# Macaron block (feed-forward, causal attention, feed-forward) on one core: evacuations moved from ScalarE to VectorE, and the last head's sums moved behind the next exponentials

## What is computed

```
x = x + 0.5 * ffn(layernorm(x))      # F1; weight rounded to -1, 0, 1 times its mean absolute value
x = x + attn(layernorm(x))           # softmax over the keys, causal
x = x + 0.5 * ffn(layernorm(x))      # F2
attn(x): kqv = x @ Wqkv + bqkv; scores = k q / sqrt(32), masked; softmax; @ v; @ Wo + bo
```

## Time and profile before

| | us |
|---|---|
| median of 3 runs | 1170.1 |
| lowest of them | 1168.0 |
| the profiled execution's own time | 1165.19 |
| its span, first to last instruction | 1163.4 |
| TensorE, ScalarE, VectorE, GpSimd busy | 1098.4, 930.6, 739.8, 344.1 |

### The profile page before, as it was taken

The page is one execution under the profiler, slowest core; times in us unless marked ns, Lnnn a source line. Parts: engine busy times, 40 slices in busy tenths (PEclk is TensorE's granted clock), DMA queues, the critical chain, the costliest instruction groups (busy, mean ns, idle before and its releaser), DMA issues.

```text
span 1163.4 us, 26100 instructions
## 1 busy us (share of the span) xinstructions
PE 1098.4 (94%) x9466; PEld 709.0 (61%) x9466; DVE 739.8 (64%) x2304; ACT 930.6 (80%) x2571; POOL 344.1 (30%) x471
## 2 busy tenths in 40 slices
PE   4688999999999999999999999999999999998896
PEld 3465655465666666675666666675666666664465
DVE  6766446479754666779754666779853666754344
ACT  1248889778998989878998989978998989989641
POOL 4731120135301232335301332335401332300253
PEclk9898989599999999999999999999999999999799
DMA  7432311111112121321112121321112111000021
GB/s 254 144 110 74 111 57 39 47 50 45 45 41 83 66 66 48 120 84 48 43 43 83 66 66 48 120 80 42 47 48 83 66 65 48 21 21 12 30 66 45
DMA packets 41967, 77.71 MB, mean 67 GB/s; under 512 B 5488, under 2 KB 11632, under 8 KB 41840
## 3 DMA queue, kind: packets, MB, share of 16 engines
q1 hardware_dynamic: 41840, 76.04, 19.5%
HBM read 49.81 MB, written 25.17 MB: 64 GB/s over the span
## 4 chain that ended last, share of the span: by engine, by line
PE 78%; ACT 10%; DVE 7%; issue 2%; POOL 2%; DMA 1%; SPq 0%; DVEq 0%; ACTq 0%; POOLq 0%
PE bank L1066 30%; PE bank L1128 12%; PE bank L1190 11%; PE bank L1162 10%; PE bank L1091 7%; ACT masked_scores L972 6%; PE bank L1083 3%; PE bank L1170 3%; DVE masked_scores L817 2%; ACT prob L1000 2%; DVE st L767 1%; DVE hn L786 1%; POOL xt L685 1%; POOL rstd L675 1%; PE bank L1143 1%
## 5 line engine op out<-in xcount | busy, mean ns | idle before, releaser
L817 DVE CUSTOM_DVE_ANT_0 masked_scores<-bank,mask 128x512 f32<-128x512 f32 (+3 forms) x768 | 379.9, 554 | 263.4 <-PE bank L1128 259.9
L972 ACT ACTIVATE masked_scores<-masked_scores,mst 128x512 f32<-128x512 f32 (+3 forms) x768 | 462.8, 607 | 20.4 <-DVE mst L817 20.3
L1000 ACT ACTIVATE prob<-bank 128x512 f32<-128x512 f32 (+1 forms) x640 | 300.1, 553 | 23.9 <-PE bank L1170 23.4
L719 POOL TENSOR_SCALAR_AFFINE_SELECT prob<-prob 128x512 f32<-128x512 f32 (+1 forms) x96 | 78.8, 821 | 414.9 <-ACT prob L1000 414.6
L1066 PE MATMUL bank<-hT,wqk 128*128 128x512 f32 x768 | 194.4, 403 | 0.0
L1128 PE MATMUL bank<-kT,qT 32*128 32x512 f32 (+2 forms) x2304 | 179.9, 387 | 15.1 <-ACT prob L1000 11.7
L1128 PEld LDWEIGHTS bank<-kT,qT 32*128 32x128 f32 x2304 | 104.7, 189 | 138.1 <-issue 66.7
L1162 PE MATMUL bank<-qT,kT 32*128 32x512 f32 (+2 forms) x2304 | 176.6, 382 | 3.1 <-DVE mst L817 2.4
L1066 PEld LDWEIGHTS bank<-hT,wqk 128*128 128x128 f32 x768 | 144.0, 192 | 38.9 <-ACT prob L1000 8.1
L972 ACT ACTIVATION_READ_ACCUMULATOR masked_scores<-masked_scores,mst 128x1 f32 x768 | 146.5, 191 | 0.0
L1162 PEld LDWEIGHTS bank<-qT,kT 32*128 32x128 f32 x2304 | 102.2, 188 | 71.0 <-issue 45.9
(11 more groups left out here) (87 smaller groups left out, 997.5 us busy)
## 6 DMA issues: line engine op xcount, KB each, us to landing
wqk<-weight_scratch SPq DMA_DIRECT2D x30, 512.0 KB, 3.3
wvo<-weight_scratch SPq DMA_DIRECT2D x20, 512.0 KB, 5.9
xt<-in_L_attn_x_dram SPq DMA_DIRECT2D x32, 256.0 KB, 4.0
residual_scratch<-xt SPq DMA_DIRECT2D x32, 256.0 KB, 2.0
xt<-residual_scratch SPq DMA_DIRECT2D x32, 256.0 KB, 2.9
out_dram<-xt SPq DMA_DIRECT2D x32, 256.0 KB, 2.1
o<-in_L_attn_Wqkv_dram SPq DMA_DIRECT2D x12, 256.0 KB, 4.1
weight_scratch<-o SPq DMA_DIRECT2D x6, 512.0 KB, 3.1
```

The lines of the kernel that those rows point to most:

```text
L719: nc.gpsimd.affine_select(out=part, in_=part, compare_op=ALU.is_ge, fill=0.0, base=0, pattern=[[0, 4], [0, m], [1, P]], channel_multiplier ...
L817: nc.vector.tensor_tensor_reduce(masked_scores[:, h, at:at + n], psum(u, h)[:, at:at + n], mask[:, off:off + n], -SCALE, BIG, ALU.add, ALU ...
L972: nc.scalar.activation(of, of, ACT.Exp, bias=mst[:, c + kc, to:to + 1], scale=-1.0, accum_out=ssum[:, c + kc, to:to + 1]).then_inc(a_free, 1)
L1000: nc.scalar.activation(prob[:, at % 2, h, off:CW], psum(("S", b, n), h)[:, off:CW], ACT.Exp, scale=SCALE)\
```

## The change

VectorE takes over four things from ScalarE: the evacuation of values (`keep_values`), the high part of outputs (`high_output`), and the high parts of the rows M and N (`row`, which makes the low part right behind, after a wait on a new semaphore `row_hi`). On VectorE the output's high part stands after the uses that are no products and before the slot's normalisations; values stand in the order of the products. On ScalarE the sums of the last head of a slot's last block now follow the next slot's exponentials. The planner `SPLIT`, which counts ScalarE's high parts, loses M and N.

```diff
-SPLIT = {u: n for n, u in enumerate([u for s in SLOTS for kinds in ("M N", "T1 T2 T3", "P") for u in s.uses()
+SPLIT = {u: n for n, u in enumerate([u for s in SLOTS for kinds in ("T1 T2 T3", "P") for u in s.uses()
...
+ROWS = {u: n for n, u in enumerate([u for u in USES if u[0] in ("M", "N")])}
...
@@ VectorE
+            def row(u, dst, scale):
+                of = psum(u)[0:4 * QPC, 0:P]
+                dve.wait_ge(ring_full, full(u))
+                nc.vector.tensor_scalar(dst[:, HI, :], of, scale, None, ALU.mult).then_inc(row_hi, 1)
+                dve.wait_ge(row_hi, ROWS[u] + 1)
+                nc.vector.scalar_tensor_tensor(dst[:, LO, :], of, scale, dst[:, HI, :].bitcast(F32), ALU.mult, ALU.subtract)\
+                    .then_inc(ring_free, 1)
+
+            def keep_values(u):
+                _, b, t = u
+                dve.wait_ge(ring_full, full(u))
+                if b and t == 0:
+                    dve.wait_ge(value_done, step(b - 1, STEPS * VG))
+                for at, to in v_parts(b):
+                    i = nc.vector.tensor_copy(to[:, t, :], psum(u)[:, at])
+                i.then_inc(v_done, 1)
+
+            def high_output(u):
+                _, b, t = u
+                at = HAT[u]
+                if at >= 2:
+                    dve.wait_ge(ring_full, full(HEAVY[at - 2]))
+                dve.wait_ge(ring_free, freed(("C", b, GROUPS - 1, t // QPC)))
+                for g, n, of in output_runs(u):
+                    i = nc.vector.tensor_copy(split_tile(u)[:, HI, g:g + n, :], of)
+                i.then_inc(o_hi, 1)
...
                 elif kind == "M":
-                    c = u[3]
-                    low(u, mrow[:, c, LO, :], psum(u)[0:4 * QPC, 0:P], mrow[:, c, HI, :], (1.0 / SCALE, ALU.mult))
+                    row(u, mrow[:, u[3], :, :], 1.0 / SCALE)
                 elif kind == "N":
-                    low(u, rrow[:, LO, :], psum(u)[0:4 * QPC, 0:P], rrow[:, HI, :])
+                    if ended(u):
+                        dve.wait_ge(rall_in, 32 * ended(u))
+                    row(u, rrow[:, :, :], 1.0)
+                elif kind == "V":
+                    keep_values(u)
...
                 for u in s.uses():
                     if u not in PRODUCTS:
                         use(u)
+                for u in (SLOTS[k + 1].uses() if k + 1 < len(SLOTS) else []):
+                    if u[0] == "O":
+                        high_output(u)
@@ ScalarE (its high(u) for M and N, keep_values and high_output are gone)
                     exponentials(b, s.step)
+                if k and SLOTS[k - 1].blocks:
+                    block_sums(SLOTS[k - 1].blocks[-1], (3,))
                 for u in s.uses():
-                    if u[0] in ("M", "N"):
-                        high(u)
-                    elif u[0] == "C":
+                    if u[0] == "C":
                         evacuate(u)
                 for u in s.uses():
                     if u[0] in ("T1", "T2", "T3"):
                         high(u)
-                for u in (SLOTS[k + 1].uses() if k + 1 < len(SLOTS) else []):
-                    if u[0] == "O":
-                        high_output(u)
                 for u in s.blocks:
                     block_sums(u, range(4) if u != s.blocks[-1] else range(3))
                 for u in s.uses():
                     if u[0] == "P":
                         high(u)
-                    elif u[0] == "V":
-                        keep_values(u)
-                if s.blocks:
-                    block_sums(s.blocks[-1], (3,))
                 for n in s.weights:
                     high_weights(n)
```

More of the change, by code:

```diff
@@ L374, in macaron_kernel @@
         ring_full, ring_free, v_done = sem("ring_full"), sem("ring_free"), sem("v_done")
-        hi_done = sem("hi_done")
+        hi_done, row_hi = sem("hi_done"), sem("row_hi")
         s_full, s_exp = sem("s_full"), sem("s_exp")
@@ L925, in high @@
                                              bias=bias_of(j, g))
-                elif kind == "M":
-                    i = nc.scalar.activation(mrow[:, u[3], HI, :], psum(u)[0:4 * QPC, 0:P], ACT.Identity, scale=1.0 / SCALE)
-                elif kind == "N":
-                    if ended(u):
-                        act.wait_ge(rall_in, 32 * ended(u))
-                    i = nc.scalar.activation(rrow[:, HI, :], psum(u)[0:4 * QPC, 0:P], ACT.Identity)
                 elif kind == "T2":
@@ L939, in high @@
                 i.then_inc(hi_done, 1)
-            def keep_values(u):
-                _, b, t = u
-                act.wait_ge(ring_full, full(u))
-                if b and t == 0:
-                    act.wait_ge(value_done, step(b - 1, STEPS * VG))
-                parts = v_parts(b)
-                for at, to in parts:
-                    i = nc.scalar.activation(to[:, t, :], psum(u)[:, at], ACT.Identity)
-                i.then_inc(v_done, 1)
             def evacuate(u):
@@ L984, in high_weights @@
                 nc.scalar.activation(home(WEIGHTS[n])[:, HI, :], raw(n), ACT.Identity).then_inc(w_hi, 1)
-            def high_output(u):
-                _, b, t = u
-                at = HAT[u]
-                if at >= 2:
-                    act.wait_ge(ring_full, full(HEAVY[at - 2]))
-                act.wait_ge(ring_free, freed(("C", b, GROUPS - 1, t // QPC)))
-                for g, n, of in output_runs(u):
-                    i = nc.scalar.activation(split_tile(u)[:, HI, g:g + n, :], of, ACT.Identity)
-                i.then_inc(o_hi, 1)
             def exponentials(b, n):
```

## The result

The changed kernel takes 1146.91 us (median of four runs, 1143.5 to 1154.08), the kernel before 1169.05 us in the runs beside it (three of 1167.37 to 1170.1 us and one of 1665.48): a ratio of 0.9838, 95% interval 0.9816 to 0.9861. The profiled execution took 1146.9 us around a span of 1145.2, where before it was 1163.4: 18.2 us less, 10.2 more than the 8 predicted. The other 4.9 of the 15 us are in the base: the median that the prediction started from stood that much above the profiled run, and no later round of the kernel before had a median over 1166.87 us.

What follows compares the result with a forecast made beforehand. TensorE, busy 94%, was taken as the bound in the long middle, ScalarE in some stretches. Terms: -7.9 gains, +0.6 VectorE, +2.8 drain, -3.5 clock, total -8 us from 1170.1, giving 1162 us; 80% range 1152 to 1173.

Steps and rivals of the forecast that it cites:

- the forecast's -4.5 and -3.5: Whole kernel: -4.5 us from all terms without the clock, and -3.5 us from fewer falls of the clock.
- the middle, +0.6 in the forecast: About 237 to 1022 us: no gain, and 0.2 us lost in each of three groups with VectorE full; bounds 0 and 1.9.
- TensorE has work without a hole worth the name: About 237 to 1022 us: TensorE read as always supplied with work, for example busy 31.28 of 33.00 us.
- one late set: Near 164 us, first batch: one late set of exponentials would start sooner, gaining 0.9 us.
- the three waits that I weighed: TensorE's waits for ScalarE's exponentials: 0.84 us at 1053.55, 1.31 at 1075.29 and 2.00 at 109.47.
- the group from 1022 us: Five slots gaining 0.3 us each and two waits 0.9 each, 3.3 us in all.
- The first stretch: 94 to 109 us, before the first attention step: ScalarE never idle, loses 2.6 us of work; 2.5 us gain taken.
- The drain: After the last attention step: high outputs wait in VectorE's queue, 2.8 us longer; bounds 1.4 and 5 us.
- The clock: Stretches at clock 0.50, some 60 us, priced at 8 to 9 us; shorter waits would save 3.5 us.
- A: Rival: every fall of the clock goes, as the waits before them shorten; 1154 us, chance 0.18.
- B: Rival: almost nothing is left, as ScalarE's relief falls mostly where TensorE has no holes; 1169 us, chance 0.22.
- C: Rival: slower, as GpSimd holds high outputs at the port shared with VectorE and its queue moves; 1178 us, chance 0.12.

Runs made afterwards that it cites:

- e1: The kernel before with only the sums of a block's last head moved behind the next exponentials; 1141.79 us, ratio 0.9784.
- e6: The kernel before with the reordering and the high parts of rows M and N on VectorE; 1141.85 us, ratio 0.9801.
- e7: The kernel before with the reordering and the value evacuations on VectorE; 1142.18 us, ratio 0.9811.
- e4: The changed kernel with unused filler products on TensorE ahead of three output products in the drain; 1145.69 us, ratio 0.9806.
- e2: The changed kernel with the reordering undone, so only the moves to VectorE remain; 1175.64 us, ratio 1.0075.
- e12: The kernel before with the reordering and two fillers ahead of each block's scores in group 1's fifth to ninth slot; 1135.24 us, ratio 0.975.
- e3: The changed kernel with the high parts of the last four output tiles back on ScalarE; 1144.71 us, ratio 0.9811.
- e9: The kernel before with the reordering and two fillers ahead of each block's scores in nine slots of groups 1 and 14; 1139.93 us, ratio 0.9776.
- e11: The kernel before with the reordering, values on VectorE and two fillers per block in group 1's fifth to ninth slot; 1138.25 us, ratio 0.9758.
- e10: The kernel before with the sums of a block's last two heads moved behind the next exponentials; 1141.65 us, ratio 0.9783.

## Why the prediction was wrong

**The total.** Predicted 8 us of gain in the span's terms, measured 18.2. By slots and by the drain experiment I split the measured change into queueing and clock. The table gives both together. Queueing: group 0 -3.4 (slots two to nine), group 1 -1.0 (slots one to six), the middle -7.6, group 14 -2.7, group 15's steps -1.2, the head -0.3, the drain +3.5: -12.7. Clock: group 0 -3.7, group 1 -7.2, group 10 -1.6, head +1.4, drain +5.6: -5.5. The splits of the head, of group 0's first and last slots, of group 1's late slots and of group 15 are estimates, since waits and stretches at 0.50 change in the same slots there. Against the forecast's -4.5 and -3.5, queueing is 8.2 us off and the clock 2.0; the middle, +0.6 in the forecast, is by itself 8.2 of it, and the other terms cancel.

**The step that failed** is the sentence "TensorE has work without a hole worth the name", and with it the costing of the middle at nothing. It was read off busy shares (31.28 of 33.00 us). The kernel had a wait for exponentials in the tenth slot of nine of the twelve middle groups, 0.81 to 0.88 us each, half of it visible as idle time and half inside the busy time of the matmuls around it: 7.7 us. Summed with the small ones it was 12.1 us with the reordering alone, 7.6 in the change. The first group of the first batch failed the same way: I priced one late set at 0.9 us, and eight slots gave 3.4. The trace of the kernel before held them: its page puts 11.7 us of TensorE's idle time ahead of the blocks' scores down to the exponentials, of which the three waits that I weighed are 4.2, and the wait view of the middle has 3.8 of the rest.

**The steps that held.** The mechanism of the reordering was the right one, and where I priced it the sizes were near: 0.9 for the second group of the first batch before its clock falls (measured 1.0), 3.3 for the group from 1022 us (2.7 in the change; 3.4 in e1, where a stretch at 0.50 of 3.4 us is missing too). Durations: high outputs 19.1 us against 17 (0.68 us for the pieces of 384 and 128 columns together, above the 0.54 taken and within its bounds), rows 17.5 against 17.5, values 24.1 against 24.6; VectorE 794.9 against 802, ScalarE 877.7 against 870. "The middle gains nothing" hid that the added VectorE work also costs there: 0.4 to 0.6 us more than in e1 in nine eighth slots, 4.5 us in all by e1's middle (772.1 us) against the change's (776.6), where I had 0.6 with a bound of 1.9. That term was undersized too, with the other sign.

**The first stretch.** I took 2.5 us off it, because ScalarE was full there. The first step came 1.1 us later in the change, 0.3 earlier in e1 and 3.7 later in e6. That lies ahead of the stretch, and in the change it goes with the clock: near 74 us the kernel before has 3.4 us at 0.50, the change and e6 have 6.8, e1 and e7 none, and the same 60 matmuls (from TensorE's 182nd on) take 10.9, 12.0, 12.0, 9.2 and 9.2 us. (Another 1.3 us in e1 and 2.7 in e6 are lost before those matmuls; no run shows why.) The block of scores behind them starts at 82.56 us before and at 83.94 in the change, and from there to the first step, with no stretch at 0.50, it is 19.76 us before, 19.80 in e1, 19.62 in e6, 19.46 in e7 and 19.44 in the change. So the values' move is worth 0.3 us there, and the rest of the 2.5 is not to be found. The waits show why. The one for the values was 0.97 us and became one of 0.25 for VectorE, and the 2.00 us of the second wait became 1.61 (1.41 in e1 and 1.40 in e7), while I had counted on both being gone or under 1 us in sum. TensorE in the change:

```profile
102.83 0.79 PE L1130 MATMUL bank<-kT,qT 32*128 32x384 f32 x9 [0.25 <-DVE mst L846]
...
109.36 1.64 PE L1130 MATMUL bank<-kT,qT 32*128 32x512 f32 x9 [1.61 <-ACT prob L1009]
```

**The drain.** The mechanism (VectorE's order: residual, then high part) is what the timeline shows, and e4 prices it: 3.5 us against 2.8, within the bounds. Missed was the clock there, 5.6 us in the profiled run and 3.1 in e2's. The term as measured, 6.6 to 9.1 us, is outside its bound of 5.

**The clock.** I took -3.5 us of an estimated 8 to 9. The 27.3 us at 0.50 in group 1 cost about 7.5 us alone (e12 against e1), so the estimate of the whole was too low. The 3.4 us at 0.50 from 801.1 us, in the middle, were not on my list at all; their absence is worth 1.6. The argument that shorter waits keep the clock is only half borne out. The wait at 204.95 us shrank from 0.84 to 0.39 us in e1, and the stretch came back from 200.3 us, 27.3 us long; in e7 the same wait is 0.38 us and none follows. In the change, e3, e4, e6, e7 and the profiles of e9, e11 and e12 it stayed away or was 3.4 us. TensorE: Matmul & The Clock Gate (Part 1: The HAM clock gate) in the Trainium skill says that activity releases the throttle. The filler runs, with mean clocks of up to 0.986, fit that. Why e1 fell and e7 did not, no run here shows.

**The rivals.** A (1154 us) had the clock partly right, but its price lay in the wrong place. B (1169) fell. C, slower through VectorE's queue and the port, did not come as a whole, though its hold by GpSimd is there. Of the 56 pieces of high outputs, 54 take 205 to 553 ns by their size. Two pieces of 128x128 take 780 and 782 ns, where the fourteen others of that size take 205 to 223. In both cases GpSimd's low part of the piece before had started 0.29 us ahead of them. Two pieces with the hold (the second of them starts at 1106.10), GpSimd beside them, and two pieces without:

```profile
1105.63 1.24 DVE L823 CAST hts<-o 128x384 fp32r<-128x384 f32 x2
1105.81 0.99 POOL L693 TENSOR_TENSOR hts<-o,hts 128x384 fp32r<-128x384 f32 x1 [5.07 <-DVE hts L823]
...
1115.10 0.68 DVE L823 CAST hts<-o 128x384 fp32r<-128x384 f32 x2
```

That is 0.56 us twice, in the last batch (1068.65 and 1106.10 us), and none of the 24 mid-kernel tiles has it. e2 shows that the moves alone are slower by 0.75%, through the drain (+6.6 us, part of it the clock), the eighth slots of the middle (+3.5) and the long stretch at 0.50 in group 14, not through this hold.

## What to carry to other kernels

Busy time of TensorE is no proof that it does not wait: compare the count of matmuls per microsecond, or the duration of the same set of matmuls between two stretches, and read the waits by releaser even where they are 0.4 us each, since nine of them with their hidden half are 7.7 us. In an in-order queue, the operation that frees a resource for the next engine goes ahead of work that nobody waits for yet; that was worth more here than moving 53 us of work to an emptier engine. And where an engine is idle at the end of the program, its place in the last chain is worth keeping: the same four tiles cost 3.5 us by the order of a queue that was 69% busy on average, and more where the clock falls in the waits.

## What the runs showed of the hardware

The clock falls at repeatable places, but not in every run. In groups 2, 6 and 10 TensorE waits 1.0 us for VectorE's reciprocal, in every kernel. The same wait in the kernel before (800.50 us, then 3.4 us at 0.50 from 801.1) and in e6 (522.52 us, then from 523.0):

```profile
800.50 0.27 PE L1143 MATMUL bank<-ident,rcol 128*16 128x128 f32 x1 [1.01 <-DVE rcol L845]
```
```profile
522.52 0.27 PE L1159 MATMUL bank<-ident,rcol 128*16 128x128 f32 x1 [1.02 <-DVE rcol L865]
```

In the kernel before, the same wait at 276.4 and 538.4 us brought no fall, in e1 and in the change none of the three did, in e6 two and in e10 all three. A fall costs 1.6 us in its slot, and where the eighth slot waits for VectorE 0.3 of it comes back. With such differences the runs of one kernel spread over 13 us and more (e3: 1136.64 us at a mean clock of 0.980, 1150.02 at 0.964), while the kernel before stayed within 5.2 us over eleven runs (1163.88 to 1169.05) and within 9.4 over eight others (1161.31 to 1170.69). A single time can thus mislead by more than the effects of the moves: groups cut at the same products of both traces, whose lengths agree to 0.05 us where nothing changed, told apart 0.1 us.
